# Moving the products with V and the out-projection within a slot's order on TensorE, and the output's copy on ScalarE

## The reference

```
for i in range(6):
    t = shift_tokens(x)                    # half of the features from the token before
    q, k, v = split(t @ Wqkv[i])           # 16 heads of 64
    q, k = rotary(l2norm(q) * qs), rotary(l2norm(k) * ks)
    # windows of 32 queries, each with its own and the preceding 32 keys
    x = softmax(8 * q @ k.T + mask) @ v @ Wo[i] + x
    t = layernorm(shift_tokens(x)) * g + b
    x = (t @ W1_a + b1_a) * gelu(t @ W1_g + b1_g) @ W2[i] + b2 + x
```

## Time and profile before

| | |
|---|---|
| median of 3 runs | 1949.55 us (1947.46 to 1950.31) |
| profiled execution, its time | 1953.01 us |
| profiled execution, its span | 1951.2 us |
| TensorE busy | 1860.3 us (95%) |
| VectorE busy | 1581.5 us (81%) |
| ScalarE busy | 1405.6 us (72%) |
| GpSimd busy | 1372.8 us (70%) |
| granted TensorE clock, mean | 0.997 |

### The profile page before, as it was taken

The page is one execution under the profiler, slowest core; times in us unless marked ns, Lnnn a source line. Parts: engine busy times, 40 slices in busy tenths (PEclk is TensorE's granted clock), DMA queues, the critical chain, the costliest instruction groups (busy, mean ns, idle before and its releaser), DMA issues.

```text
span 1951.2 us, 68794 instructions
## 1 busy us (share of the span) xinstructions
PE 1860.3 (95%) x27097; PEld 1396.0 (72%) x27097; DVE 1581.5 (81%) x3053; ACT 1405.6 (72%) x2846; POOL 1372.8 (70%) x1458
## 2 busy tenths in 40 slices
PE   5999998999999999999999999999999999999998
PEld 4777765777777777777777677777777776777774
DVE  5776777888888888888888888888888878888875
ACT  3666665577777777777777777777777777777784
POOL 4010023888898787898788987878987879878780
PEclk9999999999999999999999999999999999999999
DMA  4000001344433345333434333343343343434332
GB/s 133 1 1 0 0 0 30 92 105 106 127 87 103 96 104 127 92 92 102 103 98 127 88 102 99 101 127 93 93 103 97 102 128 83 108 94 104 95 97 68
DMA packets 193542, 171.20 MB, mean 88 GB/s; under 512 B 32304, under 2 KB 190168, under 8 KB 193240
## 3 DMA queue, kind: packets, MB, share of 16 engines
q1 hardware_dynamic: 193240, 167.02, 32.8%
HBM read 21.14 MB, written 1.05 MB: 11 GB/s over the span
## 4 chain that ended last, share of the span: by engine, by line
PE 71%; ACT 12%; issue 7%; DVE 4%; POOL 3%; SPq 2%; DMA 0%; ACTq 0%; POOLq 0%; DVEq 0%
PE bank L971 7%; PE bank L933 7%; PE bank L901 6%; PE pair_bank L949 6%; PE bank L980 5%; PE bank L959 3%; PE bank L1032 3%; PE bank L981 3%; PE bank L982 3%; PE bank L1054 3%; ACT sq L616 2%; SPq L353 2%; PE bank L818 2%; PE bank L1046 2%; PE pair_bank L940 2%
## 5 line engine op out<-in xcount | busy, mean ns | idle before, releaser
L429 POOL TENSOR_TENSOR z_raw<-rot_u,rot_v 128x256 f32<-128x256 f32 x768 | 553.4, 745 | 102.8 <-DVE rot_v L1282 97.2
L422 POOL TENSOR_TENSOR z_norm<-probs_t,z_raw 128x512 f32<-128x512 f32 x376 | 482.0, 1282 | 92.7 <-DVE probs_t L1361 87.1
L1281 DVE TENSOR_TENSOR rot_u<-bank,tabs 128x512 f32<-128x512 f32 x384 | 263.1, 685 | 168.6 <-ACT sq L616 168.4
L449 POOL TENSOR_TENSOR sqs<-sq 128x512 f32<-128x512 f32 x192 | 245.7, 1280 | 89.5 <-issue 88.6
L980 PE MATMUL bank<-x_high,w_high 128*128 128x256 f32 x768 | 301.5, 393 | 0.2 <-issue 0.2
L681 ACT ACTIVATE pair_bank<-pair_bank 128x512 f32<-128x512 f32 x192 | 111.7, 582 | 220.8 <-DVE pair_bank L1262 220.6
L1282 DVE TENSOR_TENSOR rot_v<-bank,tabs 128x512 f32<-128x512 f32 x384 | 261.4, 681 | 0.0
L616 ACT ACTIVATE sq<-bank 128x512 f32<-128x512 f32 x384 | 225.2, 588 | 49.8 <-PE bank L982 43.6
L971 PEld LDWEIGHTS bank<-probs_t,v_late 128*64 128x64 f32 x3072 | 155.0, 137 | 144.4 <-issue 144.4
L625 ACT ACTIVATE probs_t<-bank 64x512 f32<-64x512 f32 x384 | 226.7, 590 | 35.6 <-PE bank L959 33.4
L933 PE MATMUL bank<-sqs,consts 128*128 128x512 f32 x384 | 199.0, 600 | 25.4 <-POOL sqs L449 25.4
(11 more groups left out here) (181 smaller groups left out, 4555.2 us busy)
## 6 DMA issues: line engine op xcount, KB each, us to landing
zqk<-z_norm SPq DMA_DIRECT2D x1536, 64.0 KB, 2.1
v_late<-v_sb SPq DMA_DIRECT2D x192, 192.0 KB, 2.6
w_qkv<-in_L_ffn_Wqkv SPq DMA_DIRECT2D x18, 512.0 KB, 4.9
v_late<-v_sb SPq DMA_DIRECT2D x192, 32.0 KB, 2.6
wo<-in_L_ffn_Wo SPq DMA_DIRECT2D x24, 128.0 KB, 2.3
w<-in_L_ffn_W SPq DMA_DIRECT2D x12, 170.5 KB, 3.4
z_norm<-in_L_attn_x SPq DMA_DIRECT2D x4, 256.0 KB, 5.4
w_qkv<-in_L_attn_w_kv_up SPq DMA_DIRECT2D x4, 256.0 KB, 5.1
```

The source lines that it names most:

```text
L422: return pool.tensor_tensor(z_norm[:, parity, idx, :, :], rinv(m)[:, idx, :].unsqueeze(1).broadcast_to([P, 2, T]), z_raw[:, parity, idx, : ...
L429: a = pool.tensor_tensor(z_raw[:, parity, idx, half, :], rot_u[:, idx, half, :], rot_v[:, idx, 1 - half, :], ALU.add)
L1281: dve.tensor_tensor(rot_u[:, idx, :, :], src, tabs[:, 2 * idx, :, :], ALU.mult)
```

## The change

TensorE's slot begins with `turn_windows(s-1)` as before. The out-projection of group s-2 then follows at once, ahead of the scores; the products with V of group s-1 follow the scores at once, ahead of the keys; the norms then stand between keys and the MLP's products. On ScalarE the copy of the products with V moves up from behind the keys' squares to behind the exponential, ahead of the logarithm. No instruction is added or removed, and nothing else changes place.

```diff
@@ ScalarE, slot(s)
                 if three:
                     act.wait_ge(S["shifted"], s + 1)
                     act.activation(both, both, ACT.Exp).then_inc(S["raised"], 1)
+                if four:
+                    output_out(s - 1)
                 if two:
                     m = s + 3
                     act.wait_ge(S["n_done"], m + 1)
@@
                 if normed:
                     gained((s - 8) // G)
-                if four:
-                    output_out(s - 1)
@@ TensorE, slot(s)
                 if four:
                     turn_windows(s - 1)
+                if active(s, 2, GROUPS + 2):
+                    project_group(s - 2)
                 if active(s, 0, GROUPS):
                     windows(s, s // G, g)
+                if four:
+                    weigh_windows(s - 1, (s - 1) // G, (s - 1) % G, (s - 1) // G % 2)
                 if one:
                     keys(s + 4)
                 if s == 0:
                     pe.wait_ge(S["yt_ready"], STEPS)
                     project_out(B_Y)
-                if active(s, 2, GROUPS + 2):
-                    project_group(s - 2)
                 if two:
                     norms(s + 3)
-                if four:
-                    weigh_windows(s - 1, (s - 1) // G, (s - 1) % G, (s - 1) // G % 2)
```

## The result

The changed kernel takes 2099.55 us (median of 4 runs, 2096.49 to 2104.14), against 1949.93 of the kernel before, run beside it: a ratio of 1.0771, 95% interval 1.0752 to 1.0790. The profiled execution took 2098.11 us with a span of 2096.3, so its span is 145.1 longer than the 1951.2 of before. The forecast was 2062, with 2008 to 2090 as its range: the direction was right, and the size too small by 37.6 us, so that the result lies above the range.

A forecast was written before the change was run, and what follows sets the result against it. TensorE, busy 95% of the span, was taken to bound the kernel with little slack. 1953.0 plus 97 us of waits and 15 for the clock gave 2065 for the profiled execution, 2062 as median; range 2008 to 2090.

The forecast's parts named there:

- 16 plain rounds, waits: Rounds of eight slots without a layer change: 70.45 us each instead of 65.67, 4.78 longer, 76.5 us in all.
- 5 layer-change rounds, waits: Rounds at a change of layer: 71.5 us instead of 69.34, 11 us for five, bounds 5.5 and 24.
- slots 184 to 191: Seven MLP slots outside whole rounds, taken as a round without kind 4: 4.8 us longer.
- up to slot 16: The 16 slots without a full MLP wait for weights at 7.42 to 7.97: 5 us, between 3 and 11.
- clock: TensorE's clock falls in half of the 22 kind 1 slots, 1.4 us each: 15 us, bounds 0 and 37.
- VectorE's chain: Maximum, subtraction, keys' rotation and weights' multiplication come late; next turn not before 7.42 us, 7.75 in kinds 0 and 4.
- The two waits for `hidden_out`: Last TensorE products of kinds 2 and 3, centring and averaging, wait for VectorE's `hidden_out`: 0.89 us late, twice.
- Tiling: TensorE's norms followed by products of their own kind: 0.87 instead of 0.95 us, 0.08 less per slot.
- Smaller stalls: Rival: late results of kinds 2, 3, 6 and 7 come half as late, a round 2 us shorter, about 2010; chance 0.18.
- No fall of the clock: Rival: the stalls cost as worked but TensorE's clock does not fall in kind 1, 2047 us; chance 0.25.
- Faster: Rival: TensorE's own list stays the only bound, a round takes 62.8 us, 1885 in all; chance 0.04.
- More than worked, with falls throughout and the layer changes dear, 2095: Rival: total 2095 us, with clock falls throughout and layer changes costing more than worked; chance 0.05.

## Why the prediction was right in direction and short in size

The mechanism came as worked out: every wait that the prediction named is in the profile, at its place and with its releaser. The errors are in the sizes, and in waits of the layer change that it did not name. The kinds of slot, in us:

| kind | before | forecast | measured, no fall |
|---|---|---|---|
| 0 | 7.21 | 7.75 | 7.71 |
| 1 | 9.18 | 10.12 | 10.05 |
| 2 | 8.07 | 9.41 | 9.78 |
| 3 | 8.01 | 8.85 | 8.97 |
| 4 | 9.33 | 9.27 | 9.14 |
| 5 | 7.62 | 7.53 | 7.42 |
| 6 | 8.05 | 8.89 | 9.22 |
| 7 | 8.10 | 8.63 | 8.70 |

And the sum, on the scale of the span (whole rounds by the start of their first L959; falls by the longer slots of kind 1 less what kind 2 gives back):

| term | forecast | measured |
|---|---|---|
| 16 plain rounds, waits | 76.5 | 16 x (70.99 - 65.67) = 85.1 |
| 5 layer-change rounds, waits | 11 | 5 x (73.43 - 69.33) = 20.5 |
| slots 184 to 191 (one fall, in slot 185) | 4.8 | 65.0 - 57.5 = 7.5 |
| up to slot 16: slots without a full MLP, less an earlier first turn | 5 | 9.0 - 3.1 = 5.9 |
| clock | 15 | 21.2 |
| gaps inside the products with V | 0 | 6.6 |
| end | 0 | -1.7 |
| sum | 112.3 | 145.1 |

The last 4.9 us of the miss are the executions': that of before lay 3.5 above its median, that of after 1.4 below. Luck is in the sum as well: the first turn of weights, ahead of all that was changed, came at 351.6 us in this execution and at 354.6 in that of before (351.6 to 354.9 in the kept runs).

**Right.** VectorE's chain: the turn behind kind 0 was allowed at 7.75 and came at 7.71. Kind 1: the products with V were to start 4.97 us into the slot, 2.59 late; in slot 145 they start at 5.03 (recorded idle time 2.42 to 2.52). The two waits for `hidden_out`: 0.89 twice, as worked. The copy of the products with V lies in the wait for the norms in seven kinds of slot, and with the copy left late the turn waits 1.24 us: the cover is real. In kind 5 it is not there: the exponential is late and the logarithm starts right behind the copy, which TensorE does not feel but at the change of a layer.

**The layer change was the largest error.** The prediction looked for the bound of these rounds in GpSimd's 63.77 us alone and took 11 us for the five (bounds 5.5 to 24); they cost 20.5. Two lists that it had not followed there end late. In kind 3, 10.00 us instead of 8.97, it is ScalarE's:

```profile
1453.37 1.71 ACT L604 ACTIVATE tabs<-consts,par_rot 128x256 f32<-128x256 f32 x4
1454.98 0.40 ACT L645 ACTIVATE xc<-xc 128x256 f32<-128x256 f32 x1
```

and TensorE's timeline, kinds 3 and 5:

```profile
1455.43 0.70 PE L1076 MATMUL bank<-xc,consts 128*128 128x256 f32 x2 [1.88 <-ACT xc L645]
...
1472.76 0.39 PE L992 MATMUL bank<-w_high,x_high 128*128 128x256 f32 x1 [0.79 <-ACT probs L687]
```

The keys' squares come later by the keys, the rotary tables (L604) stand behind them, and the centred values' squares behind the tables. That list, with 1.71 us of extra work behind the late instruction, was in the trace of before too, in the same slots (L1076 waited 0.63 for L645 there), and was not looked at. The run with those squares ahead of the tables took kind 3 from 10.00 to 8.64.

Kind 5, 8.57 instead of 7.42, is another matter. The values wait for the logarithm, but this stands behind an exponential that had waited for VectorE, and VectorE is late since kind 4 (from the timelines of GpSimd, VectorE and ScalarE):

```profile
1461.18 1.82 POOL L417 TENSOR_TENSOR w_low<-w_qkv,w_high 128x768 fp32r<-128x768 f32 x1
...
1461.65 1.63 DVE L1308 TENSOR_TENSOR xc<-xc,rstd 128x256 f32<-128x256 f32 x1
...
1470.92 0.58 ACT L681 ACTIVATE pair_bank<-pair_bank 128x512 f32<-128x512 f32 x1 [3.65 <-DVE pair_bank L1262]
```

In all five of these rounds the 256-column product L1308 takes 1.61 to 1.63 us in kind 4 instead of 0.42, each time while GpSimd splits new weights (L417); the kernel before had 0.64 to 0.80 there. So GpSimd's extra work may count after all, through VectorE; that it is the cause is not shown.

**Kinds 2 and 6** were short by 0.37 and 0.33. Of kind 2's: the out-projection starts 1.16 us into the slot (1658.34), not 0.99, since the residual ends later by that; and TensorE loses 0.07 to 0.08 wherever it starts again after a wait: the out-projection that waited leaves 0.94 before the mask instead of 0.87, the last product leaves 0.51 before the next turn instead of 0.43. The forecast priced each restart at nothing. Four ends and two out-projections per round make 0.46, and the later residual twice 0.17: together 0.80 of the 0.89 by which kinds 2, 3, 6 and 7 are longer than worked (the other four kinds are shorter by 0.35). It fits; no run took it apart.

**The clock.** Slot 113 in three stretches: ahead of its products with V, from about their start on, and the rest:

```profile
1353.00:1357.50 4.50, 2.51 (x74) 1.94 (x74) 3.54 (x7) 4.47 (x7) 2.50 (x3) 1.00 0.37 97
1358.00:1361.40 3.40, 2.96 (x37) 2.87 (x38) 0.84 (x2) 2.76 (x4) 2.22 (x3) 0.50 0.17 42
1361.40:1364.77 3.37, 3.37 (x20) 2.40 (x19) 2.87 (x6) 2.05 (x4) 1.44 (x2) 1.00 0.34 84
```

The granted clock is at 0.50, the 1.2 GHz level, when the products with V start behind their stall, and is back at 2.4 GHz for the rest of the slot. Half of the slots of kind 1 had been taken to fall; in the whole rounds 15 of 21 did, and one of kind 6. A slot of kind 1 with a fall lasts 11.8 us on the mean, 1.8 more than one without, dearer than the 1.4 worked out. But part comes back: VectorE and ScalarE keep their pace (the sum L1267 takes 0.68 us at either level of the clock, the exponential L681 0.58), and the following kind 2 takes as little as 8.98 instead of 9.78. So 16 falls cost 21.2 us, 1.3 each: share and price of the forecast were both off, but not far. In kind 1 the stall and the fall went together across the runs: with 4.24 us of stall all 21 slots fell, with 2.4 to 2.5 between 11 and 15, with 1.81 (the copy alone, ahead of the norms) one, with 1.09 none (nor with the 0.86 of the kernel before). The whole rounds' falls in other kinds are all at a layer change. Most stand behind the wait of L1076 for L645, 1.87 to 2.21 us: all five with the products with V and the copy moved, none in the changed kernel, one to three in five other runs. Slot 62 of the changed kernel, and slot 158 of the one without Gelu, fell behind two waits of 0.77 or 0.78. The Trainium skill, "TensorE: Matmul & The Clock Gate", section "Why this matters for your kernels", with its warning of long idle gaps, was borne out in direction.

**Tiling.** The new order was credited with 0.08 per slot for one change of product kind fewer. Kind 5, without a wait, went from 7.62 to 7.42: the products with V no longer follow the norms (which take 0.86 from start to start instead of 0.95), the gate product no longer follows the products with V (2.28 from its start to the slot's end instead of 2.39), and the scores pass into the products with V without a loss (0.77 from start to start). Two borders that cost 0.1 each are gone; the bounds of 0.1 either way that the prediction gave for the border behind the scores held. The Trainium skill, "TensorEngine Tiling (Array Packing)", section "Key Properties", says that a change of tiling mode drains the engine. The traces agree with 0.1 us at these two borders; at the change from the scores to the products with V they show no loss.

**The rivals.** Smaller stalls: no; kinds 2, 3, 6 and 7, of which it spoke, came longer than worked (its "about 2010" lies between 2005 without falls and 2020 with half of them). No fall of the clock: no. Faster: the condition named, weights 6.66 us into the slot, is missed by a microsecond: L1272 ends 7.66 us into slot 144 (1646.39 and 0.69). "More than worked, with falls throughout and the layer changes dear, 2095" was nearest, and had been given 0.05. The range ended at 2090, because its bounds were taken singly, and four terms came dear together: the layer changes by 9.5 us, the plain rounds by 8.6, the gaps inside the products with V by 6.6 (they had been put at nothing) and the clock by 6.2.

## What to carry to other kernels

In a pipeline written out by hand, moving an instruction earlier on the bounding engine makes all that it passes later; follow each passed result through the other engines to the next wait, in every kind of slot and at the rare stages too, where an extra piece of work stands in the list behind it. A stall's price is not only its length: add the restart, and the clock where it is long. And try the parts apart: here the out-projection's move cost 37 us alone and saved 67 beside the others.

## What the runs showed of the hardware that was not expected

In the changed kernel TensorE stops inside an unbroken block of products with V in nine slots of the whole rounds, for 0.4 to 1.3 us each, 6.4 us in all, with the clock at its upper level and no engine that releases it (and in slots 13 to 15 ahead of these). One such place, slot 116, on TensorE's timeline:

```profile
1387.18 0.34 PE L971 MATMUL bank<-probs_t,v_sb 128*64 128x64 f32 x4 [0.25 <-issue]
```

The slots are 38 to 40, 116, 142, 143 and 166 to 168, and the runs with TensorE's moves alone, without Gelus, and with `hidden_out` moved show gaps in several of the same slots (38 or 116 or 166 in each), while the kernel before and the runs that leave the products with V last show none, and the run with the keys between scores and products one. They seem to hang on the place in the program and not on data; but the order of products directly behind the scores is not enough, since with the out-projection left behind the keys there was none either.

The record of the transfers points at the cause. The changed kernel's page has a queue of kind "instruction":

```profile
q8 instruction: 209, 3.42, 0.7%
```

Its 209 transfers of 16 KB are some 63 bytes for each of TensorE's 54194 products and weight loads, about one transfer per slot. In all twelve stops, and in all 44 of more than 0.25 us that the kept runs show, TensorE goes on 1.2 to 1.6 us after such a transfer has landed (in slot 116 it landed at 1385.81, and L971 goes on at 1387.18). By chance a landing would lie in that stretch in about one case of twenty. Scores and products with V in one piece are 192 of these instructions in 1.85 us, of about 258 in a slot. So TensorE probably stops for its own instructions. No run varied this: it is read from the traces and not shown by an experiment.

The other point is how much a fall of the clock gives back: with TensorE at half speed a slot lost 1.8 us on the mean, and the next regained up to 0.8. The waits that end that next slot are for VectorE (L1316, L1324), whose pace did not change.
